# Protein pair sums of a two-layer token mixer: quarters of 128 by 128 pairs, with the block products beside the stream

## The reference

```python
# layer 0: the pairs are normalized, projected and gated first
pp = sigmoid(_ln(protein_pair) @ gw2) * (_ln(protein_pair) @ w2 + b2)   # (256, 256, 128) -> (256, 256, 64)
ab1 = sigmoid(z @ gw1) * (z @ w1 + b1) * z_mask                         # (256, 64, 64)
block1 = einsum('bikc,bkjc->bijc', pp, ab1)
# layer 1: the pairs come raw, (256, 256, 64)
block1 = einsum('bikc,bkjc->bijc', protein_pair, ab)
```

## Time and profile before

| | us |
|---|---|
| median of 3 runs | 2685.96 (2681.09 to 2686.23) |
| the profiled execution | 2686.12 |
| its span in the trace | 2684.4 |
| PE busy | 1917.1 (71%) |
| DVE busy | 1474.2 (55%) |
| ACT busy | 1216.0 (45%) |
| POOL busy | 1187.5 (44%) |

### The profile page before, as it was taken

The page is one execution under the profiler, slowest core; times in us unless marked ns, Lnnn a source line. Parts: engine busy times, 40 slices in busy tenths (PEclk is TensorE's granted clock), DMA queues, the critical chain, the costliest instruction groups (busy, mean ns, idle before and its releaser), DMA issues. The chain is left out here.

```text
span 2684.4 us, 52043 instructions
## 1 busy us (share of the span) xinstructions
PE 1917.1 (71%) x12902; PEld 1674.4 (62%) x12903; DVE 1474.2 (55%) x6291; ACT 1216.0 (45%) x3261; POOL 1187.5 (44%) x1255
## 2 busy tenths in 40 slices
PE   6867877777683200008999999937699557999996
PEld 5756767666573200006888888835499347998995
DVE  7966584774895411113333333359622896776666
ACT  4566483663561000004555555524310465776665
POOL 3544242331892677773555555556510671001220
PEclk9988998999675555558999999967799678999998
DMA  4022231321730311112222222145562210000003
GB/s 130 0 64 76 67 106 52 94 78 34 282 129 1 105 53 51 53 52 76 71 70 71 70 71 69 45 140 165 136 156 65 80 47 7 0 0 1 0 0 126
DMA packets 248341, 193.95 MB, mean 72 GB/s; under 512 B 94328, under 2 KB 210358, under 8 KB 248254
## 3 DMA queue, kind: packets, MB, share of 16 engines
q1 hardware_dynamic: 230846, 159.08, 20.4%
q0 software_dynamic: 17408, 33.87, 3.5%
HBM read 123.09 MB, written 71.86 MB: 73 GB/s over the span
## 5 line engine op out<-in xcount | busy, mean ns | idle before, releaser
L1420 POOL DMA_INDIRECT choices<-ab_tiles x288 | 287.3, 998 | 255.2 <-ACT ab_tiles L1454 181.7
L315 POOL TENSOR_TENSOR small<-small 128x4 f32<-128x4 f32 x192 | 199.0, 1037 | 331.3 <-DVE small L308 331.3
L1334 POOL DMA_INDIRECT sorted_tokens<-work x256 | 248.0, 969 | 121.0 <-issue 80.9
L1491 PE MATMUL banks<-w,hidden 128*128 128x128 f32 x2304 | 276.3, 278 | 0.0
L1491 PEld LDWEIGHTS banks<-w,hidden 128*128 128x128 f32 x2304 | 262.6, 192 | 16.3 <-ACT hidden L1445 16.1
L1468 PE MATMUL banks<-ident,ab_tiles 128*128 128x128 f32 x288 | 44.0, 277 | 308.5 <-DMA ab_tiles<-sorted_tokens 308.5
L344 PE MATMUL banks<-ident,small 128*128 128x128 f32 x640 | 124.5, 313 | 182.2 <-ACT small L332 151.6
L1548 PE MATMUL banks<-small 128*128 128x128 f32 x1536 | 239.9, 293 | 6.4 <-DVE small L1603 3.8
L1468 PEld LDWEIGHTS banks<-ident,ab_tiles 128*128 128x128 f32 x288 | 34.5, 144 | 309.0 <-DMA ab_tiles<-sorted_tokens 308.8
L332 ACT ACTIVATE small<-small 128x128 f32<-128x128 f32 x384 | 161.6, 484 | 144.2 <-DVE small L320 143.9
L1541 PE MATMUL banks<-ab_tiles,small 128*128 (+1 forms) x1536 | 215.1, 277 | 6.2 <-DMA small<-L_ffn_V_o 6.2
(11 more groups left out here) (223 smaller groups left out, 4924.0 us busy)
## 6 DMA issues: line engine op xcount, KB each, us to landing
small<-L_conv_protein_pair SPq DMA_DIRECT2D x128, 256.0 KB
sorted_tokens<-work SPq DMA_DIRECT2D x32, 585.0 KB
ab_tiles<-sorted_tokens SPq DMA_DIRECT2D x72, 260.0 KB, 2.8
work_again<-choices SPq DMA_DIRECT2D x32, 512.0 KB, 3.8
work_again<-L_conv_protein_pair SPq DMA_DIRECT2D x32, 512.0 KB, 6.1
x_tiles<-x SPq DMA_DIRECT2D x32, 256.0 KB, 3.7
work<-x SPq DMA_DIRECT2D x32, 256.0 KB, 3.1
after_mixture<-x_tiles SPq DMA_DIRECT2D x32, 256.0 KB, 2.2
```

Source lines behind the costliest of these rows:

```text
L315: self.scaled.done(pool.tensor_tensor(self.r[:, u, :], self.var[:, u, :], self.mhalf, ALU.pow))
L1334: pool.indirect_dma_start(out=self.sorted, out_offset=bass.IndirectOffsetOnAxis(ap=where[:, u, t, k:k + 1], axis=0), in_=rows[:, u, t, k, ...
L1420: pool.indirect_dma_start(out=self.out, out_offset=bass.IndirectOffsetOnAxis(ap=rows[:, u, t, E + 1:ROW].bitcast(U32), axis=0), in_=y[:, u ...
L1491: last = pe.matmul(out[:, t * P:(t + 1) * P], hidden[:, u % 2, h, t * P:(t + 1) * P], w2[:, u % 2, h * P:(h + 1) * P], start=False, stop=h ...
```

## The change

A quarter is now 128 rows i by 128 k instead of 64 rows by 256 k: (ic, kc) in the place of (ic, h). Each channel has one product in a quarter, with 128 x 128 weights, and its result is 128 x 64; the sum over kc is made by the adds, which now run over 128 partitions. In all there are half as many products as before (256 in place of 512 in a layer), with twice the weight columns, and as many adds as before (32).

In the first layer, besides:

- The gated pairs are stored channel by channel. `by_channel(q)` sees the same buffer as c, then i, so `dest(n)` gives the sigmoid and the gate a destination whose channels stand 512 bytes apart, and the weights of a product stand one after the other.
- The four quarters are one pipeline of 128 groups, written out in full on VectorE, ScalarE and TensorE (`peel=quarters * per_chunk`). The block products are a further stage of TensorE's loop with lag 37, three channels in each step; the adds are a further stage of VectorE's loop with lag 38. The products of quarter q are so made beside the stream of quarter q + 1, and those of the last quarter after it.
- ScalarE waits before each sigmoid until the products that read the same buffer two quarters before are done.

In the second layer the products and adds keep their order; the weights stand 256 bytes apart as before, 128 of them now.

```diff
-    return Carve(chip.work)(2, ICS, C, C)
+    return Carve(chip.work)(2, P, C)
...
-def load_chunk(sp, pp, ppv, ic, h, arrived):
-    for kc in range(ICS):
-        for i in range(0, C, ROWS):
...
+def load_chunk(sp, pp, ppv, ic, kc, arrived):
+    for i in range(0, P, ROWS):
+        sp.dma_start(pp[:, 1 - kc, i:i + ROWS, :],
+                     ppv[ic * P + i:ic * P + i + ROWS, kc * P:(kc + 1) * P, :]
+                     .rearrange("i k c -> k i c")).then_inc(arrived, 16)
...
+PER_GROUP = 3
+BLOCK_LAG = 37
...
+    per_chunk = P // G
+    quarters = ICS * ICS
...
+        last_of = [-(-8 * (c8 + 1) // PER_GROUP) - 1 for c8 in range(C // 8)]
+
+        def buffer(q):
+            return pp[:, 1 - q % ICS]
+
+        def by_channel(q):
+            return buffer(q).rearrange("p i c -> p (i c)").rearrange("p (c i) -> p c i", c=C)
+
+        def dest(n):
+            i = (n % per_chunk) * G
+            return by_channel(n // per_chunk)[:, :, i:i + G].rearrange("p c i -> p i c")
+
+        def product(pe, q, c):
+            kc = q % ICS
+            return pe.matmul(chip.banks[:, 4 + c // 8 % 4, c % 8 * NC_:(c % 8 + 1) * NC_],
+                             buffer(q)[:, :, c] if raw_pairs else by_channel(q)[:, c, :], chip.ab[:, kc * NC_:(kc + 1) * NC_, 0, c], start=True, stop=True)
+
+        def accumulate(dve, ic, n, c8):
+            sums = chip.ab[:, bass.ds(ic * NC_, NC_), 1, c8 * 8:(c8 + 1) * 8]
+            blocked.ready(dve, n)
+            summed.done(dve.tensor_tensor(sums, chip.bank(4 + c8 % 4).rearrange("p (c j) -> p j c", c=8), sums, ALU.add))
...
+                def add_blocks(n, u):
+                    q, r = n // per_chunk, n % per_chunk
+                    if r in last_of:
+                        accumulate(dve, q // ICS, q * 8 + last_of.index(r), last_of.index(r))
+                engine_loop(dve, quarters * per_chunk, 4,
+                            [(lambda n, u: stream.stats(dve, n, u), 0), (lambda n, u: stream.apply(dve, n, u), 1),
+                             (lambda n, u: stream.gate(dve, dest(n), n, u), 4), (add_blocks, BLOCK_LAG + 1)],
+                            peel=quarters * per_chunk)
...
+                def squash(n, u):
+                    blocked.free(act, n // per_chunk * 8 + 7)
+                    stream.squash(act, dest(n), n, u)
+                engine_loop(act, quarters * per_chunk, 4,
+                            [(lambda n, u: stream.apply_act(act, n, u), 0),
+                             (lambda n, u: stream.keep(act, n, u), 1), (squash, 2)], peel=quarters * per_chunk)
...
+                if raw_pairs:
+                    with pe.Fori(0, ICS) as ic:
+                        for kc in range(ICS):
+                            pe.wait_ge(pp_in[kc], (ic + 1) * (16 * P // ROWS))
+                            for c in range(C):
+                                if c % 8 == 0:
+                                    summed.free(pe, (ic * 2 + kc) * 8 + c // 8)
+                                last = product(pe, kc, c)
+                                if c % 8 == 7:
+                                    blocked.done(last)
+                    return
...
+                def block_products(n, u):
+                    q, r = n // per_chunk, n % per_chunk
+                    if r == 0:
+                        stream.gated.ready(pe, (q + 1) * per_chunk - 1)
+                    for c in range(r * PER_GROUP, min(C, (r + 1) * PER_GROUP)):
+                        if c % 8 == 0:
+                            summed.free(pe, q * 8 + c // 8)
+                        last = product(pe, q, c)
+                        if c % 8 == 7:
                             blocked.done(last)
+                engine_loop(pe, quarters * per_chunk, 4,
+                            [(lambda n, u: stream.norm.turn(pe, n, u), 0), (lambda n, u: stream.project(pe, n, u), 1),
+                             (block_products, BLOCK_LAG)], peel=quarters * per_chunk)
```

More of the change, by code:

```diff
@@ L747, in _ @@
                 if raw_pairs:
-                    for q in range(1, 2 * ICS):
+                    for q in range(1, quarters):
                         blocked.free(sp, q * 8 + 7)
-                        load_chunk(sp, pp, ppv, q // 2, q % 2, pp_in[q % 2])
+                        load_chunk(sp, pp, ppv, q // ICS, q % ICS, pp_in[q % 2])
                     return
@@ L753, in _ @@
                 with sp.Fori(0, ICS) as ic:
-                    for h in range(2):
+                    for kc in range(ICS):
                         def load(m, u):
-                            kc, i = where(m, u, h)
-                            src = ppv[bass.ds(ic * P + (i + h * C), G), kc * P:(kc + 1) * P, :]
-                            stream.load(sp, [(0, src.rearrange("i k e -> k i e"))], (ic * 2 + h) * per_chunk + m, u)
+                            src = ppv[bass.ds(ic * P + m * G, G), kc * P:(kc + 1) * P, :]
+                            stream.load(sp, [(0, src.rearrange("i k e -> k i e"))], (ic * 2 + kc) * per_chunk + m, u)
                         engine_loop(sp, per_chunk, 4, [(load, 0)])
@@ L769, in _ @@
                 summed.open(dve)
[L770 to L779, removed]
-                                stream.gate(dve, pp[:, 1 - h, kc, bass.ds(i, G), :], base + m, u)
-                            engine_loop(dve, per_chunk, 4, [(lambda m, u: stream.stats(dve, base + m, u), 0),
-                                                            (lambda m, u: stream.apply(dve, base + m, u), 1), (gate, 4)])
-                        rows = slice(h * C, (h + 1) * C)
-                        for c8 in range(C // 8):
-                            n = (ic * 2 + h) * 8 + c8
-                            sums = chip.ab[rows, bass.ds(ic * NC_, NC_), 1, c8 * 8:(c8 + 1) * 8]
-                            blocked.ready(dve, n)
-                            summed.done(dve.tensor_tensor(
-                                sums, chip.banks[rows, 4 + c8 % 4, :].rearrange("p (c j) -> p j c", c=8), sums, ALU.add))
+                if raw_pairs:
+                    with dve.Fori(0, ICS) as ic:
+                        for kc in range(ICS):
+                            for c8 in range(C // 8):
+                                accumulate(dve, ic, (ic * 2 + kc) * 8 + c8, c8)
+                    return
+                stream.gated.open(dve)
+                stream.lin.fold(dve)
+                def add_blocks(n, u):
[6 more added lines that the diff above has]
+                            peel=quarters * per_chunk)
             @block.scalar
```

45 lines of the change are left out of this document (5 added, 40 removed).

## The result

| | before | after |
|---|---|---|
| median of five runs each, us | 2685.3 | 2698.7 (2694.5 to 2700.3) |
| ratio, 95% interval | | 1.0051 [1.0036, 1.0066] |
| the profiled execution, us | 2686.12 | 2699.35 |
| its span, us | 2684.4 | 2697.6 |
| PE / DVE / ACT busy, us | 1917.1 / 1474.2 / 1216.0 | 1889.7 / 1499.9 / 1246.8 |

What follows compares the result with a forecast made beforehand. VectorE bounds the first-layer stream, TensorE its products and the second layer. First layer 286.4 + 17.7 + 86.4 + 27 + 15.9 = 433.4 us against 433.3, second layer -1.3: 2685 us, no change, range 2636 to 2710.

Steps and rivals of the forecast that it cites:

- 128 groups straight: First-layer stage: one stream without turn-backs, first quarter 76.2 us plus 96 groups at 2.19 us, together 286.4 us.
- gate strided, 104 steps: First-layer VectorE: storage by channel lengthens the gate by 0.17 us in 104 steps without an add, 17.7 us.
- 24 adds: First-layer VectorE: each add in the stream waits for the chain just started, 3.6 us each, 86.4 us.
- clock: First-layer TensorE: falls to half speed over the pause after each add; 27 us for 24 adds, bounds 0 and 45.
- tail: First layer, fourth quarter: uncovered products after the last gate, 128 x 0.112 = 14.3 us, with wait and last add 15.9 us.
- the gate and L582 at twice the stride's price: Rival, first layer: ScalarE has no slack left and VectorE pays 0.17 us more, +22 us, 2707 us; chance 0.10.
- the 2.7 us that were forecast as the sign to look for: First-layer stream: VectorE idles some 2.7 us before each add, waiting for PE, if the forecast is right.
- Straight-line streams: First layer: the four quarters become one stream written out without turn-back; slow instruction fetch there was priced at nothing.
- The clock holds: Rival, first-layer stream: pauses are short enough for TensorE to keep its clock, the first layer loses 27 us, 2658 us; chance 0.17.
- the adds don't wait: Rival, first-layer stream: the order was read wrongly, 24 x 3.0 and 27 us are saved, 2586 us; chance 0.05.
- loads bound the second layer: Rival, second layer: products take 0.112 us despite the stride, so the stage takes 65 us instead of 112; 2638 us; chance 0.10.
- dearer loads: Rival, second layer: strided 128-column weight loads take 0.292 us a record, stage 150 us, 37 more, 2722 us; chance 0.10.

Runs made afterwards that it cites:

- busy ahead of the tail: The change plus overwritten TensorE products: ten in each step with an add, eight between last projection and last gate; 2669.3 us, ratio 0.9945.
- the packed sigmoid: The change with adds two steps later (lag 40) and the sigmoid written to a small packed buffer that the gate reads; 2593.5 us, ratio 0.9657.
- the by-row kernel with later adds: The change with first-layer gated pairs stored by row as before and the adds two steps later (lag 40); 2600.5 us, ratio 0.9686.

## Why the prediction was wrong

The mechanism and its place were right, and so was the sum that nearly cancels: the overlap saves some 90 us, the waiting adds take it back. What failed is the size of three terms in the first-layer stage, 433.4 us forecast and 445.2 measured. By the forecast's own terms:

| term | forecast | measured | from |
|---|---|---|---|
| 128 groups straight | 286.4 | 288.1 | 320.1 less 128 x 0.25 |
| gate strided, 104 steps | 17.7 | 26.0 | 104 x 0.25 (2.44 less 2.19) |
| 24 adds | 86.4 | 85.9 | 63.3 + 16.6, and 24 x 0.25 that they cover |
| clock | 27 | 19.2 | 419.2 less 400.0 |
| tail | 15.9 | 26.0 | 646.9 to 672.9 |

- **The tail** is the largest miss, 10.1 us. The step that failed is "128 x 0.112 = 14.3 us": that is the pitch at full clock, taken for a stretch that begins behind a pause of 1.48 us. I had priced the clock in the stream and forgotten it where nothing covers TensorE. At full clock the tail is 15.3 us (busy ahead of the tail); with it the stage would have come out at 434.5 us, as forecast, but by luck: the next two misses, of 8.3 and 7.8 us, all but cancel. The warning stood in the earlier trace rows: there the clock falls after pauses that the prediction calls "under 1.3 us", and the longest of which is 1.37 us, at 768.90.
- **The gate**, 8.3 us. The step that failed is "0.65 ns an element, so 0.17 us for the gate": it prices the strided read and takes the write as free. The read's price was right, 0.18 us of VectorE's time; the write takes 0.10 us more (the packed sigmoid), and a step grew from 2.19 to 2.44 us. The rival "the gate and L582 at twice the stride's price" (0.10, 2707 us) was right in that the write costs as well, but too high for it, and ScalarE kept some slack: it still waits 0.21 us for L320 in a step, as at 335.23. That an add's wait covers the longer gate in its own step fits the 2.59 us of idle time behind the first one; where the adds no longer wait, all 128 steps pay.
- **The clock**, 7.8 us the other way. The sign and the place were right. 24 times the 1.2 us that turn and projection lose at the low level is 28.8; the prediction took 27, between bounds of 0 and 45, and the runs give 19.2.
- **The adds**, "3.6 us for each add", measured 3.58 (85.9 over 24). Reading the order of the queues gave this one. How close the two figures come is in part the way of counting: the waits alone are 82.0 us in the change and 60.4 at full clock, 3.4 and 2.5 for each add, around the 2.7 us that were forecast as the sign to look for.

1.7 + 8.3 - 0.5 - 7.8 + 10.1 = 11.8 us, the stage's growth. **The second layer** came out as forecast: 0.217 us a record, and no measurable difference. That its granted clock would fall from 0.98 to 0.52 was not foreseen; it costs nothing there. **Straight-line streams**, priced at no stall for fetching instructions, held to 1.7 us, which is what the other terms leave over. "The clock holds", "the adds don't wait", "loads bound the second layer" and "dearer loads" fell with the rows above.

## What to carry to other kernels

When work is laid beside a stream as a further stage, ask for each instruction that consumes it how far back in the other engine's queue its producer stands, and what that queue waits for: a consumer must not wait, in its own step, for something that its engine has just begun to feed. One step more of distance, or the order of two stages, was worth some 80 us here, most of what the overlap gives. And price a layout on the engine that is the bound at that moment: the storage by channel gained 16 us of the total while the adds waited for the products (2714.8 less 2698.7), and lost 14 once they did not (2614.7 less 2600.5).

## What the runs showed of the hardware

**Strided weights don't follow the clock, packed ones do.** In the tails, eight channels of packed weights (16 records of 128 columns) take 1.79 us at a granted clock of 1.00 and 3.41 at 0.50: 0.112 and 0.213 us a record. With 128 columns 256 bytes apart it is 0.217 us at 0.50 (tail by row, second layer), and the same at 1.00: in the by-row kernel with later adds the records of a step, six in 1.45 us, start 0.217 us apart, and so do the first ones of the changed kernel's second layer. There the same time holds as many records at either clock:

```profile
1985.00:1987.00 2.00, 2.00 (x11) 2.00 (x11) 0.00 (x0) 0.00 (x0) 0.00 (x0) 1.00 0.92 211
...
1990.00:1992.00 2.00, 2.00 (x11) 2.00 (x10) 0.15 (x1) 0.00 (x0) 0.00 (x0) 0.50 0.89 203
```

At half clock the stride is nearly free. The Trainium skill (TensorE: Matmul & The Clock Gate, section LDWEIGHTS) gives the load as columns over 1.2 GHz, 107 ns here. The packed records at full clock, 0.112 us apart, agree; the strided and the half-clock ones take twice that.

**The clock can fall in the middle of gapless records, and stay down.** The tail of the change has 20.00 us of records in 20 at a clock of 0.50, the second layer 111.22 in 112 at 0.52. Both start at 1.00, behind a pause of about 1.5 us, and fall while the records already run without a gap, the second layer between 1987 and 1989 us. The kernel before makes the same pause of 1.5 us ahead of its second layer, and its clock falls there too, but is back at 1.00 from 1972 us on:

```profile
1968.00:1970.00 2.00, 2.00 (x20) 2.00 (x20) 0.00 (x0) 0.00 (x0) 0.00 (x0) 0.64 0.77 177
1970.00:1972.00 2.00, 2.00 (x21) 2.00 (x20) 0.26 (x1) 0.00 (x0) 0.00 (x0) 0.51 1.25 284
1972.00:1974.00 2.00, 2.00 (x21) 2.00 (x20) 0.42 (x1) 0.00 (x0) 0.00 (x0) 1.00 1.19 271
```

Its records have 64 columns of weights and take 0.110 us at either clock; those that did not get their clock back have 128 and take 0.213 to 0.217 us at half clock. That this is what decides was not tested. In the stream it was enough to keep TensorE busy for the clock to hold 1.00. The Trainium skill (TensorE: Matmul & The Clock Gate, What's actually happening) says that the default is the throttled state and that activity releases it. The stream and the kernel before agree; in the tail and in the changed second layer gapless records alone did not release it.

**A strided write costs VectorE time, and a strided read more.** For the 256 elements of a gate, 512 bytes apart, the write takes 0.10 us of VectorE's time and the read 0.18 (0.33, 0.43 and 0.61 us from the gate's start to the next instruction's). Its record alone would say the opposite: 416, 597 and 714 ns, so 0.18 for the write and 0.12 for the read. ScalarE's record with a strided write of the same elements is 0.23 us longer (365 to 592). The Trainium skill (SBUF — State Buffer, the note on SBUF cachelines) names a penalty for each access to a new 16-byte line, without a size; these are sizes for two engines.
